# Stacks of Q and K in one tensor, filled by 7 transfers instead of 13, and the minimum split before it is turned

## What is computed

```python
Q = einsum('bsd,hdk->bhsk', x, Wq)
K = einsum('bsd,hdk->bhsk', kv, Wk)
V = einsum('bsd,hdk->bhsk', kv, Wv)
energy = einsum('bhsk,bhtk->bhst', Q, K)
# a0, a1: lengths = number of energies of row 0 that are not 0; columns from there on are -inf
lengths = sum(energy[:, :, 0, :] != 0, axis=-1)
energy = where(cols >= lengths, -inf, energy)
# a0, a6: causal;  a2 to a5: a mask from the inputs
score = softmax(energy / sqrt(dk), axis=-1)
out = einsum('bhst,bhtk->bhsk', score, V)
```

## Time and profile before

| | |
|---|---|
| Median of 3 runs | 3566.97 us (3563.54 to 3571.05) |
| The profiled execution's own time | 3571.17 us |
| Its span, first to last instruction | 3569.3 us |
| TensorE busy | 3069.8 us, 86% |
| VectorE, ScalarE, GpSimd busy | 54%, 41%, 13% |
| Mean granted TensorE clock | 0.905 |

### The profile page before, as it was taken

One profiled execution on the slowest core, in us unless ns is written; L12 is line 12 of the kernel. 1 busy time (PEld: TensorE's weight loads), 2 busy tenths in 40 slices (PEclk: granted clock), 3 DMA queues, 4 the chain that ended last, 5 costly groups with the idle time before them and its releaser, 6 DMA issues. The chain is left out here.

```text
span 3569.3 us, 47592 instructions
## 1 busy us (share of the span) xinstructions
PE 3069.8 (86%) x16790; PEld 1814.4 (51%) x16912; DVE 1923.2 (54%) x4573; ACT 1455.1 (41%) x2134; POOL 451.6 (13%) x538
## 2 busy tenths in 40 slices
PE   6888878855999999899999999988999999784775
PEld 3444333232344444389898989963443343373443
DVE  4555777655666666443333333335777777443333
ACT  1333444431555555444444444423555554431222
POOL 0011111033112110010000000010111122121011
PEclk7888898876999999989999999998999999887777
DMA  2112121101222222000000000002222222001221
GB/s 90 47 38 54 44 65 45 33 1 41 72 66 85 59 83 57 17 24 24 25 25 25 24 25 25 1 15 57 74 81 66 77 61 52 1 1 40 52 64 40
DMA packets 95789, 158.42 MB, mean 44 GB/s; under 512 B 28520, under 2 KB 38120, under 8 KB 93368
## 3 DMA queue, kind: packets, MB, share of 16 engines
q1 hardware_dynamic: 95544, 155.24, 15.5%
HBM read 60.76 MB, written 2.10 MB: 18 GB/s over the span
## 5 line engine op out<-in xcount | busy, mean ns | idle before, releaser
L882 ACT ACTIVATE probT_a<-scores 128x1024 f32<-128x1024 f32 (+3 forms) x832 | 785.2, 949 | 1004.3 <-PE scores L738 477.4
L993 DVE CUSTOM_DVE_ANT_0 ring<-ring,maskb_a 128x512 f32<-128x512 f32 x1024 | 681.8, 716 | 211.2 <-PE ring L753 208.3
L753 PE MATMUL ring<-K_a,Q_a 64*128 64x512 f32 (+7 forms) x1664 | 466.7, 437 | 161.5 <-DMA Q_a<-fixed_a 97.3
L774 PE MATMUL outputs<-probT_a,V_a 128*32 128x512 f32 (+6 forms) x3328 | 470.9, 606 | 27.1 <-ACT oT_a L889 13.2
L1325 DVE TENSOR_TENSOR hidden_moe<-whole_moe,hidden_moe 128x512 fp32r<-128x512 f32 x288 | 199.8, 694 | 530.6 <-ACT whole_moe L1247 530.4
L1168 PE MATMUL scores<-tokens_moe,weights_moe 128*128 128x512 f32 x1728 | 455.1, 400 | 10.7 <-issue 10.7
L991 DVE TENSOR_REDUCE negm_a<-ring 128x1 f32<-128x512 f32 (+3 forms) x640 | 329.8, 561 | 237.1 <-PE ring L759 181.5
L720 PE MATMUL scores<-Q_a,K_a 64*128 64x512 f32 (+7 forms) x1664 | 425.8, 489 | 3.8
L720 PEld LDWEIGHTS scores<-Q_a,K_a 64*128 64x128 f32 (+1 forms) x1664 | 171.6, 193 | 482.6 <-issue 359.8
L1181 PE MATMUL ring<-weights_moe,hidden_moe 128*128 128x256 f32 x2592 | 402.7, 283 | 2.2 <-DVE hidden_moe L1325 1.5
L753 PEld LDWEIGHTS ring<-K_a,Q_a 64*128 64x128 f32 (+1 forms) x1664 | 243.0, 204 | 278.9 <-DMA Q_a<-fixed_a 113.5
(11 more groups left out here) (152 smaller groups left out, 3114.3 us busy)
## 6 DMA issues: line engine op xcount, KB each, us to landing
Q_a<-parts_a SPq DMA_DIRECT2D x672, 64.0 KB
K_a<-parts_a SPq DMA_DIRECT2D x672, 64.0 KB
raw<-in_moew SPq DMA_DIRECT2D x9, 2048.0 KB, 7.7
maski_a<-in_mask SPq DMA_DIRECT2D x16, 1024.0 KB, 5.2
wt<-in_w SPq DMA_DIRECT2D x7, 1024.0 KB, 4.8
Q_a<-mrow_a SPq DMA_DIRECT2D x416, 4.0 KB
kvT_a<-in_ctxT SPq DMA_DIRECT2D x12, 512.0 KB, 3.5
wrow<-in_row SPq DMA_DIRECT2D x7, 512.0 KB, 5.5
```

Source lines behind the costliest of these rows:

```text
L753: last = pe.matmul(bank("S", j, n, e)[:, 0:w], Q[rows, g, qt * P:(qt + 1) * P], K[rows, g, 0:w], start=True, stop=not a.causal)
L774: last = pe.matmul(OB[x * slot:(x + 1) * slot, q0:S], V[:, m % 2, kb, c:c + slot], probT[:, kb % 2, x, q0:S], start=(kb == 0), stop=(kb == ...
L882: act.activation(probT[:, kb % 2, 2 * p:2 * p + 2, q0:S], scores_bank(j, n)[:, :, q0:S], ACT.Exp, bias=0.0, scale=-1.0).then_inc(c_exp.sem, 1)
L993: least = dve.tensor_tensor_reduce(sc, sc, maskb[:, m % 2, qt, :], 1.0, BIG * 2, ALU.add, ALU.min, out)
```

## The change

`Q` and `K` become two halves of one tensor `stacks`, one beside the other in each partition, and `parts` is laid out as low Q, high Q, high K, low K. One transfer then fills the same rows of both: 6 transfers of 128 KB for 12 of 64 KB. The stack of j + 3 moves to half 0 of a group, ahead of the minimum rows of j + 1. Four semaphores `c_stack` take the place of two.

The minimum is split on VectorE (item "split", half 0, two operations of 128x4x4 with a drain each) into `mx`, high and low beside each other; then TensorE turns it, by 4 transposes, and ScalarE copies 8 rows of 512 (`mrow`), which 2 transfers bring into the stack. VectorE no longer takes part after the transpose.

The memsets of Q and K are gone. SyncE clears the fourth rows by a transfer of 1 MB from `fixed` (2 KB of zeros, repeated), waits for it, and then issues the static rows. TensorE no longer waits for `c_static`; ScalarE and VectorE wait for V's memset only where they first write V. In block 1 GpSimd scales the weights before it clears V, and TensorE and VectorE no longer wait for the constants at the start.

```diff
-        out += [(u * h + 1, "oT", 0, u - 1), (u * h + 1, "m", 0, u + 1),
-                (u * h + step, "mrows", 0, u + 1), (u * h + step, "stack", 0, u + 3)]
+        out += [(u * h + 1, "oT", 0, u - 1), (u * h, "stack", 0, u + 3),
+                (u * h, "split", 0, u + 1), (u * h + 1, "m", 0, u + 1), (u * h + 1, "mrows", 0, u + 1)]
...
-RINGED = {..., "m": "DD", ...}
+RINGED = {..., "m": "AA", ...}
...
+        parts = sb("parts", [P, KB, 4, S], F32R)
+        high, low = {"q": 1, "k": 2}, {"q": 0, "k": 3}
+        stacks = sb("stacks", [P, GS, 2, S], F32R)
+        Q, K = stacks[:, :, 0, :], stacks[:, :, 1, :]
+        fixed = sb("fixed", [32, 2, S], F32)
+        negm = sb("negm", [P, 3, QT, group], F32)
+        mx = sb("mx", [P, 2, QT, 32], F32R)
+        mrow = sb("mrow", [8, 2, S], F32R)
...
-                for dst, kind, order in ((Q, 0, (0, 1, 0)), (K, 1, (0, 0, 1))):
-                    for n, part in enumerate(order):
-                        for t in range(2):
-                            c = 64 * (u % 2) + 32 * t
-                            sp.dma_start(dst[n:P:4, 2 * u + t, :].bitcast(F32),
-                                         parts[c:c + 32, kind, blk, part, :].bitcast(F32)).then_inc(done, 16)
+                for n, which in enumerate((slice(1, 3), slice(0, 3, 2), slice(1, 4, 2))):
+                    for t in range(2):
+                        c = 64 * (u % 2) + 32 * t
+                        sp.dma_start(stacks[n:P:4, 2 * u + t, :, :].bitcast(F32),
+                                     parts[c:c + 32, blk, which, :].bitcast(F32)).then_inc(done, 16)
...
-                sp.wait_ge(*c_rD.at("m", j, 0))
-                sp.wait_ge(*c_mhi.at(j))
-                for part, row in ((0, ROW_HIGH), (1, ROW_LOW)):
-                    for e in range(group // 2 if group == 4 else 1):
-                        dst = Q[row + 64 * e:row + 64 * e + 1, 2 * u:2 * u + 2, :].bitcast(F32)
-                        sp.dma_start(dst.rearrange("p t (q n) -> p (t q) n", q=QT),
-                                     mrow[8 * e:8 * e + 8, j % 2, part, :].bitcast(F32)).then_inc(done, 16)
+                sp.wait_ge(*c_rA.at("m", j, 0))
+                for t in range(2):
+                    sp.dma_start(stacks[ROW_HIGH:P:32, 2 * u + t, 0, :].bitcast(F32),
+                                 mrow[4 * t:4 * t + 4, j % 2, :].bitcast(F32)).then_inc(done, 16)
...
-            sp.wait_ge(c_blank, blanks)
-            sp.dma_start(K[ROW_HIGH:P:32, :, :].bitcast(F32),
-                         same(fixed[0:4, 1, :], GS)).then_inc(c_static, 16)
-            sp.dma_start(Q[ROW_PEN:P:64, :, :].bitcast(F32),
+            sp.wait_ge(c_fixed, number + 1)
+            sp.dma_start(stacks[ROW_HIGH:P:4, :, :, :].rearrange("p g a n -> p (g a) n").bitcast(F32),
+                         same(fixed[0:32, 0, :], 2 * GS)).then_inc(c_static, 16)
+            sp.wait_ge(c_static, 48 * number + 16)
+            sp.dma_start(stacks[ROW_HIGH:P:32, :, 1, :].bitcast(F32), same(fixed[0:4, 1, :], GS)).then_inc(c_static, 16)
+            sp.dma_start(stacks[ROW_PEN:P:64, :, 0, :].bitcast(F32),
                          same(fixed[0:2, 1 if length else 0, :], GS)).then_inc(c_static, 16)
-            sp.wait_ge(c_static, 32 * (number + 1))
+            sp.wait_ge(c_static, 48 * (number + 1))
...
-                pe.wait_ge(c_const, 96)
-            pe.wait_ge(c_static, 32 * (number + 1))
...
-                    pe.wait_ge(*c_rD.at("S", j, halves - 1, 1))
-                    pe.transpose(out[0:32, 0:P], negm[:, j % 3, :], identf[:, :]).then_inc(c_ring.sem, 1)
+                    pe.wait_ge(*c_split.at(j))
+                    for qt in range(QT):
+                        last = pe.transpose(out[0:32, qt * P:(qt + 1) * P], mx[:, j % 2, qt, :].bitcast(F32),
+                                            identf[:, :])
+                    last.then_inc(c_ring.sem, 1)
...
-                    act.activation(mrow[0:rows, j % 2, 0, :], bank("m", j, 0)[0:rows, 0:P], ACT.Copy, scale=-1.0)\
-                        .then_inc(c_mhi.sem, 1)
+                    act.activation(mrow[:, j % 2, :], bank("m", j, 0)[0:8, :], ACT.Copy).then_inc(c_rA.sem, 1)
...
-            dve.memset(negm[:, :, :], 0.0)
-            dve.memset(K[:, :, :].bitcast(F32), 0.0)
-            dve.memset(Q[:, :, :].bitcast(F32), 0.0).then_inc(c_blank, 1)
+            dve.memset(mx[:, :, :, :].bitcast(F32), 0.0)
...
-                if kind == "m":
-                    rows = QT * group
-                    dve.wait_ge(*c_mhi.at(j))
-                    dve.scalar_tensor_tensor(out=mrow[0:rows, j % 2, 1, :], in0=bank("m", j, 0)[0:rows, 0:P],
-                                             scalar=-1.0, in1=mrow[0:rows, j % 2, 0, :].bitcast(F32),
-                                             op0=ALU.mult, op1=ALU.subtract).then_inc(c_rD.sem, 1)
+                if kind == "split":
+                    apart = 8 // group
+                    dve.wait_ge(*c_ring.at("m", j - 2, 0))
+                    dve.drain()
+                    dve.tensor_scalar(mx[:, j % 2, :, 0:8:apart], negm[:, j % 3, :, :], -1.0, None, ALU.mult)
+                    dve.drain()
+                    dve.scalar_tensor_tensor(out=mx[:, j % 2, :, 1:8:apart], in0=negm[:, j % 3, :, :], scalar=-1.0,
+                                             in1=mx[:, j % 2, :, 0:8:apart].bitcast(F32), op0=ALU.mult,
+                                             op1=ALU.subtract).then_inc(c_split.sem, 1)
```

70 lines of the change are left out of this document (34 added, 36 removed).

## The result

The changed kernel takes 3413.55 us (median of 4 runs, 3411.72 to 3420.81) where the kernel before takes 3569.01 us (4 runs, 3563.54 to 3573.47): 0.9569 of it, with a 95% interval of 0.9549 to 0.9589. That is 155 us less.

What follows compares the result with a forecast made beforehand. TensorE's instruction stream was taken to bound blocks 2 and 3, waits and a lowered clock blocks 1 and 4. The terms -86 - 38 + 44 - 9 = -89 us gave a median of 3478 us, range 3428 to 3530.

Steps and rivals of the forecast that it cites:

- The waits for the stack, -86: Steady parts: stack issued earlier in 7 transfers for 13, so TensorE's waits go; -86 us, bounds -60 and -96.
- rival 2: Block 4: the waits move to something else late next, only half of the 96 comes back; 3516 us, 12%.
- The clock, -9: Block 4: with waits gone, 218.5 us of matmuls run at 0.80 instead of 0.77; -9 us, bounds 0 and -20.
- The transposes, +44: All blocks: 4 transposes a group for 1 on TensorE, 0.35 us more in blocks 2 and 3, 0.45 elsewhere; +44 us.
- The split, 0 (-15 to +45): Each group: TensorE's new wait for VectorE's split, taken as covered by its ring's waits and penalty matmuls; 0 us.
- Rival 5: Each group: VectorE is behind when the split is due and TensorE stands; 3612 us at 1.2 us a group, 6%.
- The starts, -38: Block starts without stack memsets and with shorter stacks: -12.6, -7.1, -10 and -8.1 us for blocks 1 to 4.
- the zero fill, 4.2 us: Block starts: SyncE's 1 MB of zeros takes 4.2 us plus 2 us landing; alternative 8.2 us, making the starts -26.
- Block 1's first stack: Start of block 1: the first stack leaves at 28.1 us, not 36.82, and is 3.9 shorter; -12.6 us.
- the first minimum: Start of block 3: the minima wait for the mask at 2407.7 instead of the scores until 2417.80; -10 us.
- Nothing for code that is the same: Mixture of experts and feed-forward stages, untouched by the change: 0 us in the sum.
- -89: Whole kernel: sum of stack waits -86, starts -38, transposes +44 and clock -9, against the profiled 3571.2 us.

Runs made afterwards that it cites:

- the order alone: Kernel before the change, with only the stack moved ahead of the minimum rows (13 transfers, four semaphores, old minimum and starts): 3432.61 us, 0.9614.
- the run that brings back the waits of block 4 alone: Changed kernel, block 4 alone with its stack again in 12 + 1 transfers and behind the minimum rows: 3488.71 us, 0.9775.
- one to six transposes a group: Kernel before with the early stack, same transpose repeated: one 3432.61 us, two 3424.03, three 3435.63, four 3433.75, six 3436.1.
- the later transposes: Changed kernel with the transposes of the split minimum and the minimum rows one half of a group later: 3430.3 us, 0.9598.
- the run with the order taken back: Changed kernel with minimum rows and then the stack where they stood before, the stack still in 7 transfers: 3453.05 us, 0.9665.

## Why the prediction was wrong, step by step

Two terms carry most of the error: the transposes, put down as 44 us of the stage and about 6 in it, and the clock of block 4, put at 9 us and worth 30.

**The waits for the stack, -86: right.** No wait for a stack is left in a steady part, of 95.5 us before, as the sum had it, and by the reason given: the order alone does it. TensorE's idle time in the steady parts fell by 78 us, with the new waits for the split in it. Little else was late next: rival 2 did not come.

**The clock, -9: the mechanism right, the size wrong by a factor of three.** The text saw that matmuls behind waits of 2.9 us ran at the lower level, and then only moved block 4 from 0.77 to 0.80, by the likeness of block 1. It got 0.94. TensorE's busy time there fell by 30 us, and rose by 31 in the run that brings back the waits of block 4 alone. Rows 3 had a hint: behind the one shorter wait, 1.47 us, the pair showed 0.44 us, the higher level. If that level holds for nearly all groups, an estimate from the mean clocks is that 206 us of matmuls at 0.79 in the steady part are 168 at the 0.97 that it got, 38 less; busy time came out 8 above that, with 48 transposes more. Block 1, whose clock the sum left as it was, got 0.87 for 0.83, and TensorE is busy for 12 us less there in spite of 96 instructions more.

**The transposes, +44: wrong in kind.** Rows 6 gave the right busy time (0.33 us more; 0.32 measured), but it was set down as time of the stage because TensorE is busy for 92% of it. From one to six transposes a group, blocks 2 and 3 become longer by 3 us at most. Three more a group made the steady parts 6 us longer, not 44: some 38 of the error are here. That busy time fills idle time in which TensorE waits for VectorE is the step that the sum left out.

**The split, 0 (-15 to +45): a small cost in its place.** TensorE waits for it 20 times, 13.6 us, 8 times in block 3, and there a stretch of lower clock stands behind four of the waits. It is part of why block 3 became longer by 4.9 us, though the order alone makes it shorter by 14.6: the later transposes gave 9 of these 19.5 us back. Another 4.5 are the wait for the mask (L844), which belongs to the start, and the rest is open. The step looked at VectorE's order of work, not at GpSimd beside it. Rival 5's mechanism is real: up to 5.2 us a group where the split falls beside a long GpSimd operation, but not in each group.

**The starts, -38: measured -26.7.** The term at fault is the zero fill, 4.2 us assumed by the likeness of stack transfers. It took 11.75 with landing, more than even the upper bound, 8.2 and 2. One row that gave the price was of transfers that SyncE issues one after another, 64 KB each 0.62 us or 106 GB/s, and the other moved little; that 1 MB would go at 250 GB/s was in neither. Block 1's first stack left at 31.1 us, not 28.1. Blocks 1, 2 and 3 were off by 3.2, 0.2 and 1.9, block 4 by 5.8. For block 3 that flatters the forecast, which was for the first minimum: released by the mask, as it said, it came 31.6 us into the block for 35.5, 3.9 us earlier and not 10.

**Nothing for code that is the same: wrong by 10.6 us.** The mixture of experts became faster by an accident of the number of instructions ahead of it.

In sum: transposes -38, clock of block 4 -21, mixture of experts -11, the feed-forwards -1, less the starts' +11: -60 of the -61 between -89 and -150 in the profiled executions. That it closes so well is in part luck: the clock of block 1, the split and the mask of block 3 are not in it and happen to cancel, and each size is from one profile.

## What to carry over

Before a busy instruction is set down as time on an engine that is 92% busy, ask what the other 8% wait for: if it is another engine's result in each round, some work more is nearly free (here up to 0.56 us a group). A wait that is removed also gives back the clock behind it; price the matmuls of the whole stage at the level that stretches without waits show. And an issue that is late because of what stands ahead of it in its queue is mended by a change of order; the run that did only this gave 136 of 155 us.

## What the runs showed of the hardware

- A transfer of 1 MB to every fourth partition takes 11.75 us when it reads from the first 32, and 5.50 when it reads from the same fourth ones.
- A VectorE operation from SBUF to SBUF on 16 columns takes 0.18 us alone and up to 5.57 us (in the run with the order taken back) beside a GpSimd operation, with whose end it ends.
- Where TensorE's loop over an expert begins, a stop of 1.4 to 2.1 us comes once or twice, depending on the number of instructions ahead; three stops more cost 9 us, with the clock behind them.
- Transfers of 128 KB take as long to issue on SyncE as those of 64 KB, 0.61 us for 0.59 in the median.
